# Four-layer conditional transformer: q's and k's parts stored in DRAM in the order of use, and read in fewer, taller pieces

## The reference, cut to what matters

```python
h = _modulate(_ln(x), sh_msa, sc_msa)
qkv = (h @ w_qkv + b_qkv).reshape(B, N, 3, nh, hd).transpose(2, 0, 3, 1, 4)
q, k, v = (qkv[0], qkv[1], qkv[2])
attn = jax.nn.softmax(jnp.einsum('bhqd,bhkd->bhqk', q, k) * hd ** (-0.5), axis=-1)
o = jnp.einsum('bhqk,bhkd->bhqd', attn, v).transpose(0, 2, 1, 3).reshape(B, N, C)
x = x + g_msa[:, None, :] * (o @ w_proj + b_proj)
...
attn = jnp.einsum('nthd,ntkd->nthk', q * scale, k)   # layer 3
```

## Time and profile before

| what | us |
|---|---|
| three timed runs | 1608.52, 1612.34, 1615.13 (median 1612.34) |
| the profiled execution's own time | 1615.5 |
| its span, first to last instruction | 1613.7 |
| PE busy | 1441.4 (89%) |
| DVE, ACT, POOL busy | 1039.2, 780.9, 543.7 |
| mean granted clock of TensorE | 0.943 |

### The profile page before, as it was taken

How to read it: one execution, slowest core, us unless ns; L and a number is a source line. 1 busy time by engine, 2 the same in 40 slices (tenths; PEclk the granted TensorE clock), 3 DMA queues, 4 the chain that set the end, 5 groups by cost and what they waited for, 6 DMA issues and landing times. The chain is left out here.

```text
span 1613.7 us, 41194 instructions
## 1 busy us (share of the span) xinstructions
PE 1441.4 (89%) x15976; PEld 1082.4 (67%) x15976; DVE 1039.2 (64%) x2592; ACT 780.9 (48%) x1287; POOL 543.7 (34%) x739
## 2 busy tenths in 40 slices
PE   6789988999999998988999678787999798988998
PEld 2467666777777775766777467665776576666776
DVE  4678875666767666878447688886445565655342
ACT  2367654333323326766545366664544354645443
POOL 3345532211131303544334224433334243432321
PEclk9799999999999998999999789999999799988999
DMA  4765631111122214555011433443208576785021
GB/s 129 147 148 141 153 85 51 49 42 42 34 75 60 59 42 96 135 125 121 17 30 45 105 88 90 116 108 82 43 23 111 85 100 112 117 118 98 11 67 45
DMA packets 210858, 134.95 MB, mean 84 GB/s; under 512 B 144189, under 2 KB 193048, under 8 KB 204458
## 3 DMA queue, kind: packets, MB, share of 16 engines
q1 hardware_dynamic: 190706, 129.75, 37.0%
q10 hardware_dynamic: 19960, 2.57, 1.3%
HBM read 98.24 MB, written 33.24 MB: 81 GB/s over the span
## 5 line engine op out<-in xcount | busy, mean ns | idle before, releaser
L1532 DVE TENSOR_REDUCE negm<-banks 128x8 bf16<-128x1024 f32 x256 | 311.4, 1216 | 110.8 <-PE banks L650 108.4
L1223 ACT ACTIVATE prob<-banks 128x1024 f32<-128x1024 f32 x256 | 262.2, 1024 | 244.9 <-PE banks L672 244.2
L1949 POOL TENSOR_TENSOR X<-X,gx 128x288 f32<-128x288 f32 x128 | 104.9, 832 | 303.6 <-DVE gx L1562 301.7
L1350 ACT ACTIVATE hid<-banks 128x512 f32<-128x512 f32 x144 | 85.9, 597 | 230.5 <-PE banks L951 230.5
L650 PE MATMUL banks<-qk 54*128 54x128 bf16 (+1 forms) x2048 | 125.3, 245 | 65.5 <-DVE negm L1532 22.0
L668 PE MATMUL banks<-qk 54*128 54x128 bf16 (+1 forms) x2048 | 173.3, 239 | 8.6 <-ACT prob L1223 5.0
L967 PEld LDWEIGHTS banks<-wfc,hid 128*128 128x128 f32 x1152 | 156.6, 190 | 29.9 <-issue 19.9
L672 PE MATMUL banks<-mT,identb 64*128 64x128 bf16 x2048 | 170.2, 229 | 2.1 <-issue 2.1
L967 PE MATMUL banks<-wfc,hid 128*128 128x144 f32 x1152 | 161.1, 286 | 0.0
L950 PE MATMUL banks<-hT,wfc 128*128 128x512 f32 x288 | 149.4, 600 | 1.6 <-DMA wfc<-in_L_cond_w 1.1
L684 PE MATMUL banks<-prob,V 128*32 128x128 f32 x4096 | 150.5, 292 | 0.0
(11 more groups left out here) (165 smaller groups left out, 2822.8 us busy)
## 6 DMA issues: line engine op xcount, KB each, us to landing
qk<-qk_scr SPq DMA_DIRECT2D x336, 72.0 KB
gbuf<-gate_scr SPq DMA_DIRECT2D x64, 288.0 KB, 4.5
qk_scr<-parts SPq DMA_DIRECT2D x48, 288.0 KB, 3.0
qk<-qk_scr SPq DMA_DIRECT2D x48, 216.0 KB
qk<-cw_scr SPq DMA_DIRECT2D x8, 1024.0 KB, 4.6
qk<-tok_scr SPq DMA_DIRECT2D x112, 72.0 KB
qk_scr<-parts SPq DMA_DIRECT2D x48, 144.0 KB, 2.8
qk<-qk_scr SPq DMA_DIRECT2D x48, 144.0 KB
```

Source lines behind the costliest of these rows:

```text
L1223: act.activation(prob[:, 2 * (U % 3):2 * (U % 3) + 2, :], pairs[1][:], ACT.Exp, scale=scale).then_inc(a_exp, 1)
L1532: dve.tensor_reduce(negm[:, u // 2, :, 4 * (u % 2):4 * (u % 2) + 4], pairs[0][:].rearrange("q s (h k) -> q s h k", k=T), AX.X, ALU.max, ne ...
L1949: pool.tensor_tensor(x, x, gx[:, q, :, :], ALU.add).then_inc(g_x, 1)
```

## The change

In layers 0 to 2 the DRAM scratch `qk_scr` gets six part places for a side instead of three, in the order in which they stand in `qk`. `RUNS` says which parts, as (first, how many): q has parts 0 1, 0 1 2, 0, and k has 0 1 2, 0, 0 1, so the six products are the same and stand in another order. A write of one piece of `parts` becomes three, and a half's side is read in two pieces, 48 rows (`EVEN`) and 6. In layer 3 `tok_scr` is as before, and a side's half is read in three runs of parts, of which k's were single parts before. `written` and `fetched` count the semaphores' new steps.

```diff
+RUNS = (((0, 2), (0, 3), (0, 1)), ((0, 3), (0, 1), (0, 2)))
 KS = 6 * D
+EVEN = KS // 16 * 16
...
-        qk_scr = nc.dram_tensor("qk_scr", [2, 2, 3, D, H, TG], BF16, kind="Internal").ap()
+        qk_scr = nc.dram_tensor("qk_scr", [2, 2, 6, D, H, TG], BF16, kind="Internal").ap()
...
         def written(n):
-            return 64 * (n + 1) if n < 24 else 64 * 24 + 192 * (n + 1 - 24)
+            return 192 * (n + 1)
 
         def fetched(n):
-            return 144 * (n // 3 + 1)
+            i = n // 3 + 1
+            return 64 * i if n < 24 else 64 * 8 + 96 * (i - 8)
...
                         if l < 3:
-                            sp.dma_start(qk_scr[p, side, :, a:b].rearrange("a d h t -> (d h) a t"), src).then_inc(q_w, 16)
+                            at = 0
+                            for first, many in RUNS[side]:
+                                sp.dma_start(qk_scr[p, side, at:at + many, a:b].rearrange("a d h t -> (d h) a t"),
+                                             src[:, first:first + many]).then_inc(q_w, 16)
+                                at += many
                             continue
...
                 for s in range(2):
-                    r0 = 64 * s
-                    for part in range(3):
-                        rows = (3 - part) * D
+                    for side, runs in enumerate(RUNS):
+                        row = 64 * s
                         if l < 3:
-                            q_src, k_src = (qk_scr[p, side, :, :, 8 * s:8 * s + 8].rearrange("a d h t -> (a d) (h t)")
-                                            for side in range(2))
-                            q_dst = qq[r0:r0 + rows, r].rearrange("r h t -> r (h t)")
-                            k_dst = kk[r0:r0 + rows, r].rearrange("r h t -> r (h t)")
-                        else:
-                            q_src, k_src = (tok_scr[p, side, 2 * s:2 * s + 2].rearrange("c b a d h w -> (a d) (c b) (h w)")
-                                            for side in range(2))
-                            q_dst, k_dst = qq[r0:r0 + rows, r], kk[r0:r0 + rows, r]
-                        sp.dma_start(q_dst, q_src[0:rows]).then_inc(q_r[r][s], 16)
-                        for i in range(3 - part):
-                            sp.dma_start(k_dst[D * i:D * i + D], k_src[D * part:D * part + D]).then_inc(q_r[r][s], 16)
-                        r0 += rows
+                            src = qk_scr[p, side, :, :, 8 * s:8 * s + 8].rearrange("a d h t -> (a d) (h t)")
+                            dst = qk[row:row + KS, side, r].rearrange("r h t -> r (h t)")
+                            for part in (slice(0, EVEN), slice(EVEN, KS)):
+                                sp.dma_start(dst[part], src[part]).then_inc(q_r[r][s], 16)
+                            continue
+                        for first, many in runs:
+                            src = tok_scr[p, side, 2 * s:2 * s + 2, :, first:first + many] \
+                                .rearrange("c b a d h w -> (a d) (c b) (h w)")
+                            sp.dma_start(qk[row:row + many * D, side, r], src).then_inc(q_r[r][s], 16)
+                            row += many * D
```

## The result

The changed kernel takes 1594.18 us (median of 4 runs, 1584.04 to 1601.59) where the kernel before takes 1610.43 beside it (4 runs, 1606.91 to 1615.13): ratio 0.9888, 95% interval 0.9847 to 0.9928. The profiled execution takes 1596.98 us with a span of 1595.2, 18.5 us less than before's span of 1613.7.

A forecast was written before the change was run, and what follows sets the result against it. PE, busy 89% of the span, was taken as the bound, with gains only in its waits for `qk_scr` and `tok_scr` reads. 19.4 us (layers 0 to 2) plus 8.5 (layer 3) off 1615.5 gave 1588 us, range 1573 to 1605.

The forecast's parts named there:

- Reads of layers 0 to 2, "5.0 us shorter": `qk_scr` reads: busiest engine carries 16 rows instead of 24, so a read falls from 17.3 to 12.3 us.
- 0 if the rate is set by something other than the number of engines: Lower bound on the shortening of `qk_scr` reads in layers 0 to 2; the upper was 9.5 us.
- the rival of longer packets: Packets lengthen as more engines run; reads lose only 2.5 us, gain some 10.5 us, time 1605; chance 0.12.
- Writes, "1.0 us longer": Layers 0 to 2: twelve write issues instead of four lengthen a block's chain by 1.0 us (0.7 to 2.9), n = 2's by 3.0.
- the rival of slow issues: SP's twelve write issues take 1.0 us each and block the chain: slower, 1627 us; chance 0.05.
- Waits, 14.2 us off in layers 0 to 2: PE's waits for `qk_scr`: 12.2 us off at n = 2, 7, 15, 23 and 2.0 off the seven short ones.
- Clock, 5.2 us: PE's clock stays up behind the waits of n = 7 and 15, saving 2.6 us at each.
- Layer 3, "I take 1.5", 8.5 us in all: Twelve reads instead of 18 shorten a read 1.5 us; 2.5 us at three long waits, half of the short ones' 2.0.
- paid twice: Layer 3: shorter reads also land v's transfer sooner and bring the next block's writes forward, 1.0 us more per long wait.
- Sum: Whole kernel: 19.4 us from layers 0 to 2 plus 8.5 from layer 3, 27.9 us off, to 1588 us.

The follow-up runs named there:

- e4: The changed kernel, but in layers 0 to 2 a half's side read in one transfer of 54 rows instead of 48 and 6: 1576.7 us, 0.9804.
- e1: Against the kernel before: reads by runs of 18, 27 and 9 rows in all layers, three part places and four writes kept: 1571.49 us, 0.9769.
- e12: The kernel before with the same 18 read transfers, those of the two halves issued in turn in all layers: 1562.37 us, 0.9701.
- e5: The kernel before with only the twelve writes to six places in layers 0 to 2, its 18 reads kept: 1643.67 us, 1.0191.
- e3: The changed kernel with layer 3's reads as in the kernel before, so only layers 0 to 2 changed: 1611.25 us, 1.0021.
- e2: The changed kernel with layers 0 to 2 as in the kernel before, so only layer 3's reads changed: 1591.3 us, 0.989.
- e9: The changed kernel with the transfers of both halves issued in turn, in layer 3 too: 1580.66 us, 0.9813 to the kernel before.
- e6: The changed kernel, but a half's side read as 45 and 9 rows instead of 48 and 6: 1595.06 us, 0.9898 to the kernel before.
- e7: The kernel with runs of parts in all layers, its transfers to the two halves issued in turn: 1550.98 us, 0.9615 to the kernel before.
- e10: The changed kernel, but in layers 0 to 2 a half's side read in six transfers of 9, every sixth row: 1713.77 us, 1.0635.
- e11: The changed kernel, but in layers 0 to 2 a half's side read in six transfers of 9 neighbouring rows: 1673.45 us, 1.0392.
- e8: The kernel with runs of parts in all layers, plus four unawaited 48-row DRAM-to-DRAM transfers behind the reads of blocks 0 to 15: 1584.32 us, 0.9833.

## Why the prediction was right, and where it was not

The time (1594 for 1588, range 1573 to 1605) and the direction are right, and the reads got shorter and PE's waits in front of L650 with them, as forecast. But it is luck that the time is so near: 19.4 of the 27.9 us were to come from layers 0 to 2, and nothing did. By its steps:

*Reads of layers 0 to 2, "5.0 us shorter".* They are 3.1 us shorter (17.4 to 14.3). The step scaled the transfer by the rows of the busiest engine, 16 for 24. Sixteen engines came, but the row time rose from 0.60 to 0.72 us, and e4 gets 13.9 us out of nine. The term was mis-sized and its reason was wrong: the shortening comes with fewer and larger transfers (e4 against before), and with all six places in DRAM or with three (e1, 14.9) it is nearly the same. I had named the bound ("0 if the rate is set by something other than the number of engines") and the rival of longer packets, at 0.12, which for layers 0 to 2 is what happened. With nine engines the rate goes with the rows that are in flight at one time (e12 against before).

*Writes, "1.0 us longer".* 1.2 measured from the first write of the last 96 rows, 1.7 from the last parts, within the bounds of 0.7 to 2.9; at n = 2 the read starts 2.1 us later (85.85 to 87.98), for 3.0. An issue takes 0.44 us for the 0.33 assumed. So a block's way from parts to landing got 1.4 to 1.9 us shorter, not 4.0. What the writes cost alone e5 shows: 1.9%. That an issue of 2.35 us met a full queue, as the rival of slow issues has it, no row shows.

*Waits, 14.2 us off in layers 0 to 2.* In the profile -10.7 (20.6 to 9.9); n = 2 gave 0.35 for 2.0, n = 15 0.2 for 2.2 and n = 23 2.3 for 4.0. Only n = 7's is gone as forecast, and not for the reason given: its read lands when it did before (224.00 for 223.88), and PE comes 1.65 us later. A wait that shrinks because PE is late gains nothing.

*Clock, 5.2 us.* Neither came whole: n = 15 still waits 2.0 us, and the half clock that n = 7's wait brought is brought by the stop in front of 219.05 instead. PE's busy time did not fall by the 5 us forecast but by 0.3.

*Layer 3, "I take 1.5", 8.5 us in all.* The read is 3.6 us shorter (18.2 to 14.6), outside the upper bound of 2.0 that I had built from six issues; the waits fell by 14.4 us. Issues alone can't give that: the time lay in how the small transfers of neighbouring rows move, which e12 shortens nearly as much by their order alone (18.2 to 15.1). That a shorter read is paid twice is borne out: from n = 27 to 29 PE gained 7.2 us more (7.96 to 15.15), 3.1 of them before n = 29's first read (1388.64 for 1399.72), where I had 1.0, and 4.1 in the read. The step came out at about twice its size, while that for layers 0 to 2 gave nothing.

*Sum.* 19.4 + 8.5 was forecast; e3 and e2 measured 1.0021 and 0.989, so layers 0 to 2 gave nothing (3 us slower, within -1 and +8) and layer 3 gave 17.7 us (12.7 to 22.5). In sum some 18 us of the 27.9 forecast came (0.9888), and that this is near enough for the range is the work of two errors of opposite sign. No step of the prediction had the stops of PE, +9.4 us in this profile (and the clock behind them), which took what layers 0 to 2 had gained.

*The stops themselves.* In one profile of each kernel, stops over 1 us without a releaser sum to 14.8 us in the changed kernel, 13.0, 15.0 and 7.6 in e3, e9 and e6, whose reads use 16, 16 and 15 engines; to 5.4 before and 2.0, 5.1, 1.2, 3.2, 2.6, 0, 0 and 0 in e1, e2, e4, e5, e7, e12, e10 and e11, whose reads use nine; and to 0 in e8, where 16 engines carry traffic from DRAM to DRAM. The large sums go with reads on 16 engines into SBUF, and not with crowding in one half (e9); e6's 7.6 is not far from the 5.4 before. In the transfer records each of the 33 stops of all fourteen profiles ends 1.2 to 1.9 us after the end of a 16 KB packet of the queue that brings instructions (in the changed kernel the packets of 169.97, 663.83 and 691.07 end at 171.43, 665.30 and 692.72, and PE goes on at 172.95, 666.80 and 694.27). A run has 129 such packets, and at most eight are followed by a stop. That fits PE waiting for instructions whose packets come late beside the reads' packets, on engines that a nine-engine transfer leaves alone, but this is argued and not shown, and e8's traffic on all 16 engines speaks against its simplest form. No run here moves that queue, and with one profile each, the sums may vary. The cause stays open.

The Trainium skill (DMA: Bandwidth & Descriptors, how many engines) states that a transfer uses the largest k up to 16 that divides its rows; the shares of 0.55 to 0.59 where all rows go by nine and 0.85 to 1.06 with 48 rows agree. The Trainium skill (SBUF — State Buffer, "Can I just issue two DMAs to hit both halves?") answers that question with no, since two transfers at partitions 0 and 64 gained only 6% over one. Here e12 takes a read from 17.4 to 14.5 us, 17% less, by no more than alternating the halves, so on many queued transfers the measurement decides against it. By the same page's port swizzle four neighbouring rows share a port. Worked out from its table, an estimate, nine neighbouring rows reach three ports and nine rows that lie six apart reach seven, which would fit the 0.72 and 0.45 us of e11 and e10; no run shows the ports themselves.

## What to carry to other kernels

Before adding engines to a transfer, see whether its packets get longer when more of them run, and change the order of the same transfers (here, rows 0 to 63 and 64 to 127 in turn), which costs nothing and gave 3.0% alone and 3.85% with fewer transfers. When a change takes waits away and the time doesn't follow, compare when the waiting engine comes to the same instruction in both profiles: a wait can vanish because the engine is late. Then sum the stops for which the profile names no releaser, and look at the clock behind them. Split a change of two parts before crediting either: here one part gave everything and the other nothing, while the time looked as forecast.

## What the runs showed of the hardware

- Rows of 8 KB from DRAM into SBUF occupy an engine, in the mean, for 0.45 to 0.49 us with nine engines where the transfers are of rows apart (e10), of 54 rows (e4) or to both halves in turn (e7, e12); for 0.53 as runs of parts (e1), 0.60 in before's order and 0.72 as transfers of nine neighbours (e11); and for 0.72 with 16 engines, 0.69 with the halves in turn (e9).
- SP needs 0.68 us to issue a transfer of every sixth row (median of 576, rows stepped in DRAM and in SBUF) and 0.32 us for one of nine neighbouring rows: here steps between rows double the issue.
- Stops of PE with no releaser of 1 to 4 us each (longest 4.03 in e6), 13 to 15 us in a run, where reads into SBUF use 16 engines; the half clock stood behind some of them for 3.4 to 6.8 us. Each stop ends 1.2 to 1.9 us after the end of a packet of the instruction queue.
